# Reading edge targets and sources from one-value tables in the matrix build of a graph network kernel

## The reference

```
d_v = segment_sum(hyperedge_weight[he_idx], node_idx, num_segments=num_nodes)
he_feat = segment_sum(x_prime[node_idx], he_idx, num_segments=num_he)
out = segment_sum(he_feat[he_idx], node_idx, num_segments=num_nodes)
```

## Time and profile before

| | |
|---|---|
| median of three runs | 6723.85 us |
| profiled execution, its own time | 6730.24 us |
| its span in the trace | 6728.5 us |
| mean granted TensorE clock | 0.805 |
| PE / DVE / ACT / POOL busy, share of the span | 60% / 49% / 18% / 45% |
| DMA, mean over the span | 100 GB/s |
| matrix build, from DVE's first operation to its last | 1629.7 to 2597.7 us |
| first DVE operation of the next stage | 2606.0 us |

### The profile page before, as it was taken

One profiled execution on the slowest core, in us unless ns is written; L12 is line 12 of the kernel. 1 busy time (PEld: TensorE's weight loads), 2 busy tenths in 40 slices (PEclk: granted clock), 3 DMA queues, 4 the chain that ended last, 5 costly groups with the idle time before them and its releaser, 6 DMA issues. The chain is left out here.

```text
span 6728.5 us, 101449 instructions
## 1 busy us (share of the span) xinstructions
PE 4012.2 (60%) x17222; PEld 2420.5 (36%) x17251; DVE 3279.4 (49%) x11280; ACT 1187.3 (18%) x3845; POOL 3044.2 (45%) x3024
## 2 busy tenths in 40 slices
PE   2600510002676777876877999566666567777777
PEld 1300300000111112434454456343443357666665
DVE  5967920003555555443122033544444557788783
ACT  0000000000111110001012022100000156666652
POOL 0027877770000003874750000377777447777750
PEclk9999999999656557888975999555555589999995
DMA  8611112217111114655732856111111234444450
GB/s 128 88 37 48 40 50 54 54 51 23 70 62 70 62 70 157 204 178 173 258 107 100 311 192 199 44 53 52 53 52 53 46 108 130 125 126 127 124 103 19
DMA packets 717405, 673.00 MB, mean 100 GB/s; under 512 B 487624, under 2 KB 616377, under 8 KB 698166
## 3 DMA queue, kind: packets, MB, share of 16 engines
q1 hardware_dynamic: 607526, 442.47, 23.8%
q0 software_dynamic: 109568, 227.77, 12.2%
q10 hardware_dynamic: 144, 1.28, 0.1%
HBM read 528.30 MB, written 142.96 MB: 100 GB/s over the span
## 5 line engine op out<-in xcount | busy, mean ns | idle before, releaser
L488 POOL DMA_INDIRECT gathered<-node_table,idx x576 | 621.3, 1079 | 1174.9 <-ACT idx L476 1015.5
L863 POOL DMA_INDIRECT bucketed_edges<-edge_rows,idx x784 | 822.9, 1050 | 681.6 <-issue 663.3
L1329 POOL DMA_INDIRECT gathered<-node_table_xq,idx x832 | 798.5, 960 | 377.3 <-issue 225.0
L360 POOL DMA_INDIRECT gathered<-node_table,idx x816 | 771.0, 945 | 285.4 <-issue 203.3
L375 PE MATMUL ps<-onehots,gathered 128*128 128x128 f32 x1632 | 642.5, 500 | 422.0 <-DMA gathered<-node_table,idx 421.4
L1239 PE MATMUL ps<-onehots 128*128 128x512 bf16 x1152 | 573.3, 571 | 263.6 <-DVE onehots L1266 253.6
L435 PE MATMUL ps<-gathered,junk 128*128 128x512 f32 x1182 | 608.1, 623 | 90.2 <-DMA gathered<-edge_counts 90.0
L375 PEld LDWEIGHTS ps<-onehots,gathered 128*128 128x128 f32 x1632 | 408.1, 312 | 656.4 <-DMA gathered<-node_table,idx 656.1
L1157 PE MATMUL ps<-tabs,ones 49*128 49x416 f32 x4 | 3.1, 938 | 707.1 <-DVE tabs L1112 707.1
L1264 DVE TENSOR_SCALAR onehots<-iota_b,side_rows,bF 128x128 bf16<-128x128 bf16 x722 | 227.2, 315 | 396.9 <-issue 207.3
L971 POOL MEMSET agg<- 128x6400 f32 x4 | 21.7, 5432 | 848.5 <-ACTq L81 848.5
(11 more groups left out here) (358 smaller groups left out, 7719.2 us busy)
## 6 DMA issues: line engine op xcount, KB each, us to landing
gathered<-edge_counts SPq DMA_DIRECT2D x99, 1280.0 KB
edge_counts<-gathered SPq DMA_DIRECT2D x49, 1280.0 KB
gathered<-edge_counts SPq DMA_DIRECT2D x56, 896.0 KB
bucketed_edges<-edge_rows SPq DMA_DIRECT2D x52, 544.0 KB, 12.1
edge_rows<-bucketed_edges SPq DMA_DIRECT2D x208, 128.0 KB
gathered<-edge_counts SPq DMA_DIRECT2D x48, 512.0 KB
side_rows<-edge_counts SPq DMA_DIRECT2D x48, 512.0 KB
gathered<-node_table,idx POOLq DMA_INDIRECT x1392
```

The lines of the kernel that those rows point to most:

```text
L360: nc.gpsimd.indirect_dma_start(g[:, k, :], None, table, bass.IndirectOffsetOnAxis(m.idx[:, k:k + 1], 0)).then_inc(S["landed"][k], 16)
L488: nc.gpsimd.indirect_dma_start(g[:, k, :], None, a.table, bass.IndirectOffsetOnAxis(m.idx[:, k:k + 1], 0)).then_inc(S["landed"][k], 16)
L863: nc.gpsimd.indirect_dma_start(a.bucketed, bass.IndirectOffsetOnAxis(m.idx[:, k:k + 1], 0), m.erow[:, k, :], None).then_inc(S["scattered"] ...
L1329: nc.gpsimd.indirect_dma_start(g[:, k, :], None, a.table2, bass.IndirectOffsetOnAxis(m.idx[:, k:k + 1], 0)).then_inc(S["landed"][s], 16)
```

## The change

Before the walk over the blocks DVE copies the targets and the sources into tables of their own, 836 words each, one value per tile place: the targets into a free part of `m.gather`, the sources into a free part of `m.side`. L1264 and L1266 (L1267 and L1269 after the change) read their per-partition scalar from these tables.

```
+    targets, sources = m.gather[:, 8 * BT:9 * BT + 4], m.side[:, 3 * (BT + 4) + KW:4 * (BT + 4) + KW]
...
             step(V.tensor_copy(iotaK, iotaI))
+            step(V.tensor_copy(targets, m.meta[:, :, 1]))
+            step(V.tensor_copy(sources, m.meta[:, :, 2]))
...
-                            V.tensor_scalar(ohs[h], m.iotab[:, :], m.meta[:, bass.ds(t + h, 1), 2], m.bF[:, bass.ds(b, 1)],
+                            V.tensor_scalar(ohs[h], m.iotab[:, :], sources[:, bass.ds(t + h, 1)], m.bF[:, bass.ds(b, 1)],
                                             ALU.subtract, ALU.is_equal)
-                            V.tensor_scalar(ohd[h][:, 0:w], iotaK[:, 0:w], m.meta[:, bass.ds(t + h, 1), 1], -float(k0 * KB),
+                            V.tensor_scalar(ohd[h][:, 0:w], iotaK[:, 0:w], targets[:, bass.ds(t + h, 1)], -float(k0 * KB),
                                             ALU.subtract, ALU.is_equal).then_inc(S["ready"], 1)
```

More of the change, by code:

```diff
@@ L63 @@
 assert (P - 1) * NT + SPLIT * U == E and 0 < SPLIT < NI
-assert M <= KW <= NB * P and (NB - 1) % CR == 0 and (NB - 1) % 2 == 0 and 3 * NB * NR <= BT and NB % GB == 0 and NPC % RING == 0 and NCH == MB
+assert M <= KW <= NB * P and (NB - 1) % CR == 0 and (NB - 1) % 2 == 0 and 3 * NB * NR <= BT and 2 * KW <= 8 * BT and 9 * BT + 4 <= U3 * 2 * D and NB % GB == 0 and NPC % RING == 0 and NCH == MB
 class Names:
```

## The result

| | before | after |
|---|---|---|
| median of 4 runs each, us | 6723.42 (6721.93 to 6726.43) | 6636.47 (6633.61 to 6641.28) |
| span of the profiled execution, us | 6728.5 | 6639.2 |
| matrix build, barrier to barrier | 976.0 | 916.3 |
| attention stage (L1452 and its neighbours) | 1114.2 | 1080.8 |
| edge sorting stage (L893 and behind) | 1134.6 | 1138.1 |

The ratio of the times is 0.9853, 95% interval 0.9824 to 0.9882. The kernel became faster by about 87 us, where 39 us were forecast. The span shrank by 89.3 us: 59.7 in the matrix build and 33.4 in the attention stage, while edge sorting took 3.5 us more. No other stage moved by more than 1.2 us. So there are two questions: why the build gained 60 instead of 39 us, and why a stage that the diff doesn't touch gained 33.

A forecast was written before the change was run, and what follows sets the result against it. DVE's own queue was taken to bound the matrix build. Terms of -28.9 - 12.0 + 1.5 = -39.4 us took the profiled 6730.24 to 6690.8; as that execution lay 6.4 us above the median, the forecast was 6685, 80% range 6660 to 6708.

The forecast's parts named there:

- The bound: Matrix build: DVE's own queue, its waits and register operations, sets the pace in all three parts, not PE.
- The lone register operation: In front of the second L1266 of each pair: its removal saves 80 ns in 361 pairs, 28.9 us.
- what its packed group costs beyond that is covered: L1266's packed group, shrinking from six operations to five, hides behind L1264's 315 ns, so it gains nothing.
- The second packed group: In front of L1264: shrinks to three operations and 67 ns, saving 34 ns in 354 pairs, 12.0 us.
- The first packed group: In front of L1264: stays at six operations and 173 ns, so it gains nothing.
- the factor 3: Rival: the multiplication by 3 makes the packed groups slow; without it 53 us more are saved, 6632 us; chance 0.07.
- The copies: Two DVE copies of 128 x 836 ahead of the build's walk, each waited for: +1.5 us, bounds 1.4 and 2.
- 12 us in either direction for place: Queue pauses of 0.25 us in some 48 odd-body pairs may come or go as code moves: 6665 to 6700.
- a rival for place: The odd body's pauses of 0.25 us per pair spread to all 313 other pairs: 78 us slower, 6763; chance 0.05.
- the stages behind keep their lengths: Expected sign: the build shrinks by about 39 us while later stages change by no more than a few us.
- The real wait for PE: Rival: DVE truly waits for PE in 215 wide pairs, losing 24.5 us of gain, 6709.5; chance 0.08 with queue ahead.
- the queue that is ahead: Rival: DVE's register work is done ahead and covered, so only the copies count, 6725; chance 0.08 with PE wait.

The follow-up runs named there:

- after + 2: The changed kernel with two memsets of 128 x 1 on DVE behind the matrix build's walk; 6727.17 us, ratio 0.9962 to the kernel before.
- the block's value taken once: The changed kernel with the value copied once per block into a fixed column that the source one-hots read; 6577.1 us, ratio 0.974 to the kernel before.

## Why the prediction was wrong

- **The bound** was right. DVE's queue set the pace before, and still does after: each piece of register work that left made the pair shorter, in four kernels. PE kept up: none of the 722 waits held DVE's queue before, and one, by some 40 ns, after.
- **The lone register operation** was right: 28.9 us forecast. The step at h = 1 fell from 395 to 296 ns, of which 22 ns is the packed group: 0.077 x 361 = 27.8 us. The row of 30.0 us carried it, and it is 0.0 now.
- **The step that failed in the build** is the sentence "what its packed group costs beyond that is covered". I had taken the first one-hot's 315 ns as a floor, because in the earlier trace rows L1266 started just when L1264 ended. It was a coincidence of two lengths: the queue's own time was 318 ns (22 after the start, 40, 32, 173, and 51 to the next start). With 151 ns for the packed group it is 296, and the second one-hot starts while the first still runs. That term, valued at nothing, was 2 x 0.022 x 361 = 15.9 us.
- **The second packed group** was a little small: 64 ns after, not 67, so 40 ns per pair and 14.2 us for 12.0.
- **The first packed group**, six operations before and after, stayed at 173 ns, as forecast. The group with five went to 151. What makes such groups slow isn't the factor 3: with a factor 2 they take 173 as well.
- **The copies** were right: +1.5 us by their durations.
- **Two small terms** were missing: the loop's register operation (1.8 us), and seven register operations less on L1267 in the block in front (722 of ALU_OP where the earlier trace rows has 729), 7 x 0.077 = 0.5 us.
- **Sum of the build:** -27.8 - 15.9 - 14.2 - 1.8 - 0.5 + 1.5 = -58.7, measured -59.7. Of the 1.0 us between, the copies' net 0.6 in place of 1.5 explains 0.9.
- **The attention stage** is the other failed step. I allowed 12 us in either direction for place, from pauses of 0.25 us (in some 48 pairs; there are 56), and wrote a rival for place only on the slow side. The pauses that the change met were 3.4 us long, 24 of them, and they were in the trace of before, in a row that the prediction doesn't use, since the stage was unchanged. Of some 74 us of idle time that went (82.4 + 29.1 - 37.8), 33.4 came out of the stage's length. My sign that "the stages behind keep their lengths" was wrong. That the shift fell on the good side is luck: with two instructions more on DVE ahead of the loop the 33 us would not have come, as after + 2 shows. What the change itself is worth is the build's 59.7 us.
- **The real wait for PE and the queue that is ahead** both fail. For the second I had inferred from the Trainium skill, Perfetto Trace Analysis, "Sequencer Loop", that register work would be done ahead. The trace agrees with what the page says, that engine instructions are pushed into a queue and control instructions start at once: the next register operation begins 22 ns after the start of a one-hot that runs for 315. My inference was what failed. In a pair of part 0 the queue's own work fills 2.23 us against 1.33 us of the four operations, so it never gets ahead, and 44.7 us went from register work alone.
- **Of the error of 48.5 us** (6685 less 6636.5), 33.4 is place and about 20 the build, of which 18.1 are the two mis-sized terms (15.9 and 14.2 less 12.0); edge sorting gave 3.5 back.

Open: why packed groups that hold an operation on two registers behind a constant are so slow (151 ns with five operations, 173 with six, against 86 for five of another form); which places of the code are bad. 1498, 1500 and 1628 were good for the attention loop, which is 326 instructions long, and 1502, 1508 to 1512, 1516 and 1540 bad. Twelve kernels are too few to say more than that a shift of two instructions decides. Why edge sorting varies by some 10 us between kernels (1133.3 to 1143.3) wasn't studied.

## To carry to other kernels

Where an engine is idle and its waits end at "issue" or at something long over, count what its queue does per instruction and compare starts with starts: a duration of an operation is a floor only if some row shows its successor held by it. An index by register costs register work each time: take out strides and fixed values that a plain table or one copy can hold. And a change of the number of instructions moves all loops behind it, so look through the whole trace of before for long pauses at "issue", and at the packets that load instructions, and allow what they are worth in both directions.

## What the runs showed of the hardware

- The attention loop, with the same code, can run without pauses at one place and pause two instructions further: 31 packets on the queue that loads instructions against 151, and none or 24 pauses of 3.4 to 4.5 us (82.4 to 107.5 us in total), each behind the branch back to the loop's start.
- In loops over pairs the pauses are shorter, 0.1 to 0.4 us, and stay in front of the same place of the program (464) while the code is moved past it.
- DVE's operations overlap at their ends: a successor starts 0.29 us after the start of an operation of 0.31 us, without anything between them in the timeline.
- Packed groups of the one form took 151 ns with five operations and 173 with six; the others on this line 64 with three, 82 with four and 86 with five.
- PE's mean granted clock in the build rose from 0.59 to 0.67 after, and 0.73 with the block's value taken once, a mix of the levels of 1.2 and 2.4 GHz; a matmul of 128x512 took 525 ns on average after, not 571. It came along with the gain, as PE had shorter gaps between its matmuls, and was not its source: before, none of the 722 waits for PE held DVE's queue, so faster matmuls could not have shortened the build.
